# Expert layer of an attention and mixture-of-experts network on 16-bit high and low parts, first product with its weights stationary

## What is computed

```python
def _L0_ffn_ref(x, wg1, bg1, wg2, w_in, w_out):
    E, H, K, G = (8, 512, 2, 64)
    xt = x.reshape(-1, d)                     # 2048 rows, d = 256
    g = jax.nn.gelu(xt @ wg1 + bg1, approximate=False)
    logits = g @ wg2
    probs = jax.nn.softmax(logits, axis=-1)
    top_vals, top_idx = jax.lax.top_k(probs, K)
    gates = jnp.zeros_like(probs).at[jnp.arange(n)[:, None], top_idx].set(top_vals)
    h = jax.nn.gelu(jnp.einsum('nd,edh->enh', xt, w_in), approximate=False)
    o = jnp.einsum('enh,ehd->end', h, w_out)
    y = jnp.einsum('ne,end->nd', gates, o)
...
    x = x + _L0_xattn_ref(_layernorm(x, axis=-1), ctx_768, ...)
    x = x + _L0_ffn_ref(_layernorm(x, axis=-1), L0_ffn_wg1, L0_ffn_bg1, L0_ffn_wg2, L0_ffn_w_in, L0_ffn_w_out)
    x = x + _L1_xattn_ref(_layernorm(x, axis=-1), ctx_768, ...)
    x = x + _L1_ffn_ref(_layernorm(x, axis=-1), L1_ffn_w_gate, L1_ffn_w_up, L1_ffn_w_down)
```

## Time and profile before

| | us |
|---|---|
| median of 3 runs | 1109.73 |
| lowest and highest | 1107.92, 1112.27 |
| the profiled execution | 1105.96 |
| its span (first to last instruction) | 1104.2 |
| expert layer: first DMA, first matmul of the tile loop, last `copy_y`'s start | 524.27, 584.27, 722.02 |
| PE busy in the span | 914.9 (83%) |
| DVE, ACT, POOL busy | 782.2, 745.7, 623.5 |

### The profile page before, as it was taken

How to read it: one execution, slowest core, us unless ns; L and a number is a source line. 1 busy time by engine, 2 the same in 40 slices (tenths; PEclk the granted TensorE clock), 3 DMA queues, 4 the chain that set the end, 5 groups by cost and what they waited for, 6 DMA issues and landing times. The chain is left out here.

```text
span 1104.2 us, 23943 instructions
## 1 busy us (share of the span) xinstructions
PE 914.9 (83%) x9014; PEld 698.9 (63%) x9014; DVE 782.2 (71%) x1550; ACT 745.7 (68%) x1254; POOL 623.5 (56%) x571
## 2 busy tenths in 40 slices
PE   5887998999999999997518999967888989960686
PEld 4655686767676777675417999955566767760344
DVE  5768778777877786676894444458978786639676
ACT  3387888698878887882533444445797878924686
POOL 2177766776686666772515555333686767813232
PEclk9899999999999999998758999988998999975899
DMA  9479999899989979994912222182899979943011
GB/s 265 164 127 193 160 157 152 153 171 151 163 145 184 158 149 152 149 175 65 321 67 73 77 75 75 58 282 43 173 187 173 168 145 172 173 78 114 6 35 39
DMA packets 433744, 153.57 MB, mean 139 GB/s; under 512 B 406592, under 2 KB 424192, under 8 KB 433600
## 3 DMA queue, kind: packets, MB, share of 16 engines
q1 hardware_dynamic: 429888, 141.82, 66.6%
q0 software_dynamic: 3744, 10.23, 2.9%
HBM read 38.62 MB, written 12.71 MB: 46 GB/s over the span
## 5 line engine op out<-in xcount | busy, mean ns | idle before, releaser
L477 POOL TENSOR_TENSOR A_PHL<-A_pr,A_PHL 128x508 f16<-128x508 f32 x256 | 295.2, 1159 | 134.5 <-ACT A_pr L754 133.6
L753 ACT ACTIVATE A_PHL<-A_ps,A_negmax 128x508 f16<-128x508 f32 x256 | 179.6, 701 | 17.9 <-DVE A_negmax L1003 15.3
L477 POOL TENSOR_TENSOR C_PHL<-C_pr,C_PHL 128x512 f16<-128x512 f32 x128 | 150.5, 1186 | 58.0 <-ACT C_pr L754 57.5
L754 ACT ACTIVATE A_pr<-A_ps,A_negmax 128x508 f32<-128x508 f32 x256 | 181.5, 709 | 0.0
L1003 DVE TENSOR_REDUCE A_negmax<-A_ps 128x2 f32<-128x1016 f32 x128 | 154.3, 1205 | 0.0
L598 PE MATMUL A_ps<-A_K,A_Q 64*128 64x512 f32 x768 | 124.1, 427 | 12.4 <-ACT A_pr L754 9.8
L616 PE MATMUL A_ps<-A_VH,A_PT 128*128 128x65 bf16 (+1 forms) x1024 | 109.5, 197 | 18.9 <-DMA A_PT<-A_PHL 18.6
L616 PEld LDWEIGHTS A_ps<-A_VH,A_PT 128*128 128x128 f16 (+1 forms) x1024 | 93.6, 98 | 47.7 <-DMA A_PT<-A_PHL 29.6
L617 PE MATMUL A_ps<-A_VL,A_PT 128*128 128x64 f16 (+1 forms) x1024 | 108.6, 194 | 0.0
L618 PE MATMUL A_ps<-A_VH,A_PT 128*128 128x65 bf16 (+1 forms) x1024 | 108.3, 195 | 0.0
L753 ACT ACTIVATE C_PHL<-C_ps,C_negmax 128x512 f16<-128x512 f32 x128 | 88.7, 693 | 15.1 <-DVE C_negmax L1003 14.5
(11 more groups left out here) (355 smaller groups left out, 2681.8 us busy)
## 6 DMA issues: line engine op xcount, KB each, us to landing
A_PT<-A_PHL SPq DMA_TRANSPOSE x256, 3.4
M_WINl<-in_L_ffn_w_in SPq DMA_DIRECT2D x4, 1024.0 KB, 11.9
M_WOUTl<-in_L_ffn_w_out SPq DMA_DIRECT2D x4, 1024.0 KB, 12.5
C_yc<-routed_rows SPq DMA_DIRECT2D x8, 512.0 KB, 5.2
ct_split<-A_CT SPq DMA_DIRECT2D x4, 768.0 KB, 4.1
C_CT<-ct_split SPq DMA_DIRECT2D x4, 768.0 KB, 8.0
M_rows<-M_xn SPq DMA_DIRECT2D x4, 512.0 KB, 9.0
out<-X SPq DMA_DIRECT2D x16, 128.0 KB, 1.7
```

The costliest lines, as they stand in the source:

```text
L477: pool.tensor_tensor(PHL[:, e % PRING, 1, 0:KEYS], pr[:, e % RING, 0:KEYS], PHL[:, e % PRING, 0, 0:KEYS], ALU.subtract).then_inc(pl_ready. ...
L753: a.activation(PHL[:, e % PRING, 0, 0:KEYS], o, ACT.Exp, bias=nm[:, n % 4, h:h + 1])
L754: a.activation(pr[:, e % RING, 0:KEYS], o, ACT.Exp, bias=nm[:, n % 4, h:h + 1]).then_inc(p_ready.sem, 1)
```

## The change

The weights' parts become 16-bit (high float16, low bfloat16). They no longer are split in place: the loads go to a ring `raw` of 8 parts (4 loads), and loads 4 to 7 wait until earlier parts are split. The rows are split while they still lie in SBUF (`xhl`, 8 pairs of tiles), and turned by 8 DMA transposes on SP's queue, two after each of the first four loads; the rows in DRAM are high and low side by side, the same bytes as before. POOL makes 7 of the 16 low parts, DVE 9. In the tile loop a gathered tile (128 x 512, 16 bit) is turned by one DMA transpose on SP (39 of them). `expert_in` takes a 128 x 128 block of `WIN` as the stationary operand, at a register address, and moves the 128 turned rows: 24 matmuls of 128 columns in place of 6 of 512. Its output has the hidden numbers on the partitions, so that `turn_h` goes; ACT and DVE split it from SBUF. `expert_out` keeps its 12 matmuls of 256 columns, now 16-bit. PE does expert_in(s), expert_out(s-2).

```diff
-    RING, AHEAD = 3, 4
+    RING, AHEAD, XRING, HRING, IN_BANKS = 4, 4, 4, 3, 3
+    OUT_LAG, BACK_LAG = 2, 3
+    RAWS, PAIRS, SETS = 8, TILES // 2, 4
...
-        rows = nc.dram_tensor(f"{tag}_rows", [TILES * P, D], F32).ap()
+        rows = nc.dram_tensor(f"{tag}_rows", [TILES * P, 2 * D], F16).ap()
...
-        WIN = [sb(f"WIN{s}", [P, E, KC, H], FR) for s in "hl"]
-        WOUT = [sb(f"WOUT{s}", [P, E, HC, D], FR) for s in "hl"]
+        WIN = [sb(f"WIN{s}", [P, E, KC, H], dt) for s, dt in (("h", F16), ("l", BF16))]
+        WOUT = [sb(f"WOUT{s}", [P, E, HC, D], dt) for s, dt in (("h", F16), ("l", BF16))]
+        raw = sb("raw", [P, RAWS, KC * H], F32)
...
-        BY_POOL = 6
+        BY_POOL = (0, 1, 2, 4, 6, 8, 10)
...
+            def load_w(k):
+                (W, name), e = LOADS[k]
+                if k >= RAWS // PAIR:
+                    n = PAIR * (k - RAWS // PAIR + 1)
+                    sp.wait_ge(w_split, lows(n, True))
+                    if lows(n, False):
+                        sp.wait_ge(w_split_v, lows(n, False))
+                j = PAIR * k % RAWS
+                sp.dma_start(raw[:, j:j + PAIR, :].rearrange("p e (c n) -> p e c n", n=w[name].shape[3]),
+                             w[name][e:e + PAIR].rearrange("e p c n -> p e c n")).then_inc(w_loaded[k % SETS], 16)
+
+            def turn_rows(p):
+                sp.wait_ge(rows_split, p + 1)
...
+                sp.dma_start_transpose(out=XT[:, b % 2, t:t + 2, :, :].rearrange("p t k n -> p (t k) n"),
+                                       in_=xhl[:, 2 * p:2 * p + 2, :, :].rearrange("p t s d -> p (t s d)")).then_inc(xt_loaded[p % SETS], 16)
...
+            def turn_x(i):
+                sp.wait_ge(xg_loaded[i % AHEAD], 16 * (i // AHEAD + 1))
+                if i >= XRING:
+                    sp.wait_ge(in_filled, i - XRING + 1)
+                sp.dma_start_transpose(out=xgT[:, i % XRING, :, :], in_=xg[:, i % AHEAD, :]).then_inc(gt_loaded[i % XRING], 16)
+
+            for i in range(NT):
+                turn_x(i)
...
+            def expert_in(i):
+                expert[i] = pe.value_load(etab[0:1, i:i + 1], min_val=0, max_val=E - 1)
+                pe.wait_ge(gt_loaded[i % XRING], 16 * (i // XRING + 1))
+                if i >= IN_BANKS:
+                    pe.wait_ge(h_ready, i - IN_BANKS + 1)
+                for c in range(HC):
+                    for kc in range(KC):
+                        last = three(ps[:, IN_BANK + i % IN_BANKS, c * P:(c + 1) * P],
+                                     [a[:, bass.ds(expert[i], 1), kc, c * P:(c + 1) * P].rearrange("p o n -> p (o n)") for a in WIN],
+                                     [xgT[:, i % XRING, s * KC + kc, :] for s in range(2)], kc == 0, kc == KC - 1)
+                last.then_inc(in_filled, 1)
...
-            for s in range(NT + 3):
+            for s in range(NT + OUT_LAG):
                 if s < NT:
-                    turn_in(s)
-                if 1 <= s <= NT:
-                    expert_in(s - 1)
-                if 2 <= s <= NT + 1:
-                    turn_h(s - 2)
-                if s >= 3:
-                    expert_out(s - 3)
+                    expert_in(s)
+                if s >= OUT_LAG:
+                    expert_out(s - OUT_LAG)
...
+            def h_high(i):
+                a.wait_ge(h_ready, i + 1)
...
+                a.activation(hhl[:, i % HRING, 0, :].bitcast(BF16), hf[:, i % HRING, :], ACT.Copy).then_inc(h_hi, 1)
...
             def h_low(i):
-                v.wait_ge(ht_hi, i + 1)
...
+                v.wait_ge(h_hi, i + 1)
+                v.tensor_tensor(hhl[:, i % HRING, 1, :], hf[:, i % HRING, :], hhl[:, i % HRING, 0, :].bitcast(BF16),
+                                ALU.subtract).then_inc(h_split, 1)
```

More of the change, by code:

```diff
@@ L1139, in mixture @@
         xn_ready = sem("xn_ready")
+        rows_hi = sem("rows_hi")
+        rows_split = sem("rows_split")
         rows_stored = sem("rows_stored")
-        xt_filled = sem("xt_filled")
-        xt_hi = sem("xt_hi")
-        xt_split = sem("xt_split")
+        xt_loaded = [sem(f"xt_loaded{k}") for k in range(SETS)]
         z_filled = sem("z_filled")
@@ new lines, in _ @@
+            load_w(0)
+            turn_rows(0)
+            turn_rows(1)
+            load_w(1)
+            turn_rows(2)
+            turn_rows(3)
+            load_w(2)
+            turn_rows(4)
+            turn_rows(5)
+            load_w(3)
+            turn_rows(6)
+            turn_rows(7)
+            for b in range(B):
+                store_rows(b)
+            for k in range(4, len(LOADS)):
+                load_w(k)
+            def turn_x(i):
[3 more added lines that the diff above has]
+                sp.dma_start_transpose(out=xgT[:, i % XRING, :, :], in_=xg[:, i % AHEAD, :]).then_inc(gt_loaded[i % XRING], 16)
@@ L1237, in _ @@
                 gather(i)
-            pool.wait_ge(table_ready, 1)
-            for s in range(NT + 4):
+            pool.wait_ge(table_ready, 3)
+            for s in range(NT + BACK_LAG):
                 if s + AHEAD < NT:
                     gather(s + AHEAD)
-                if s >= 4:
-                    scatter(s - 4)
+                if s >= BACK_LAG:
+                    scatter(s - BACK_LAG)
         @block.tensor
@@ L1329, in expert_in @@
-            def expert_in(i):
-                pe.wait_ge(gt_split, i + 1)
-                if i >= 2:
-                    pe.wait_ge(h_ready, i - 1)
-                for kc in range(KC):
-                    last = three(ps[:, IN_BANK + i % 2, :], [a[:, i % 2, kc, :] for a in xgT],
-                                 [a[:, bass.ds(expert[i], 1), kc, :].rearrange("p o n -> p (o n)") for a in WIN],
-                                 kc == 0, kc == KC - 1)
-                last.then_inc(in_filled, 1)
@@ L1351, in expert_out @@
                 for c in range(HC):
-                    last = three(ps[:, Y_BANK + i % 2, 0:D], [a[:, i % 2, c, :] for a in hT],
+                    last = three(ps[:, Y_BANK + i % 2, 0:D],
+                                 [hhl[:, i % HRING, 0, c * P:(c + 1) * P].bitcast(BF16), hhl[:, i % HRING, 1, c * P:(c + 1) * P]],
                                  [a[:, bass.ds(expert[i], 1), c, :].rearrange("p o n -> p (o n)") for a in WOUT],
@@ L1430, in _ @@
+            for s in range(NT):
+                gelu(s)
+                h_high(s)
             a.wait_ge(l_sub, 1)
@@ L1484, in _ @@
             ch.link(v.tensor_scalar(y.bitcast(I32), two.bitcast(I32), -1.0, float(0x5F3759DF), ALU.mult, ALU.add))
-            for _ in range(3):
+            row_low(1)
+            normalised(2)
+            for k in range(3):
                 ch.link(v.tensor_tensor(two, y, y, ALU.mult))
```

275 lines of the change are left out of this document (115 added, 160 removed).

## The result

| | us |
|---|---|
| before, median (lowest to highest, 4 runs) | 1108.83 (1104.75 to 1112.27) |
| after, median (lowest to highest, 4 runs) | 1138.18 (1135.26 to 1142.24) |
| ratio after to before, 95% interval | 1.0265, 1.0232 to 1.0297 |
| profiled execution of after, its span | 1135.38, 1133.6 |

The change makes the kernel slower by 2.65%, some 29 us. The forecast was 1115, the range 1108 to 1129. The changed kernel was timed in one call only; where a later run is set against its 1138.18, the two come from different calls.

The account below looks back on a forecast made before the run. PE's sequencer, slowed by register addresses, was to bound the tile loop at 3.65 us a tile; loop +6.8, ahead of it -0.4, end -1.5, together +4.9, gave 1115 us, range 1108 to 1129.

Parts of the forecast that it names:

- The array, the sequencer's mechanism: Tile loop: PE's sequencer needs 3.65 us a tile for register instructions, above the array's 2.65; loop +6.8 us.
- The first rival: Tile loop: register steps overlap, the array stays the bound, 2.7 to 3.0 us a tile, whole 1082; chance 0.11.
- the second: `expert_in`: register-addressed stationary loads at 0.11 a pair, 3.95 us a tile, whole 1126; chance 0.17 together with a shallow queue.
- the tail of the earlier trace: Last tile before the change, PE empty: seven register steps 0.80 to 0.86 us apart, taken as 0.115 a step.
- Ahead of the loop: Loads, eight transposes and stores in turn on the DMA queue, then DVE's chain; loop starts at 583.9, -0.4 us.
- The size of a tile: Tile loop: eight groups 1.89, `expert_out` 0.90, expert read 0.75, semaphore 0.11: 3.65 us, ends 3.54 and 3.95.
- The slow rival ahead of the loop: Ahead of the loop: transposes slower than 1.76 us, sharing DMA engines with loads and stores; +5, whole 1120; chance 0.12.
- The end: After the last `expert_in`: three `expert_out` at 1.31 and 1.05 to the copy's end, 4.9 against 6.4 us; -1.5.
- PE's busy share: Sign in the tile loop: falls from 100% to some 75%, with short idle times before each group put down to issue.

Follow-up runs that it names:

- The runs at fixed addresses: Changed kernel always taking expert 0's weights at a fixed address, in the second product (1101.43 us), the first (1093.18) or both (1089.60).
- the run with the low parts dealt out otherwise: Against the kernel with WG split early, weights moving and PE turning the hidden rows: low parts 9 and 11 later on DVE, 12 on POOL; 1103.28 us.
- WG early: Changed kernel with DVE's two instructions splitting the router's weights moved from behind the seventh pair of rows to behind the second; 1126.64 us, ratio 1.0148.
- the run with both products at fixed addresses: Changed kernel with both expert products always taking expert 0's weights at a fixed address, the expert's read kept on PE; 1089.60 us, one run.

## Why the prediction was wrong

In the profile the expert layer grew by 23.3 us, where +4.9 was forecast. Of the 18.4 us between, 10.3 lie ahead of the loop and 8.1 in it.

**The array, the sequencer's mechanism: right.** The forecast's theory was that the array gets its work too late because of the register instructions, with the array's own price at 2.65 us. The runs at fixed addresses show both: 2.65 with the first product's register work gone, 3.01 with two thirds of all register instructions left, 3.84 with all. The first rival (the array bounds) and the second (dear register-addressed loads) fell. The view was the tail of the earlier trace rows: seven steps with an empty PE.

**Ahead of the loop: the step that failed.** The sum had loads and transposes one behind the other as if the queue always had something to issue, and said of load 4 "it lands at 556.2 to 560.8", that is 31.9 to 36.5 us after the layer's first DMA. It landed after 42.5. The sum left out a wait that the code shows: the transpose of rows 4 needs `z_filled`, the gate's first product, and with it WG's split, which the change put behind nearly all of DVE's row work; and SP has loads 3 to 7 queued behind that wait. Moving two small DVE instructions brought load 4 to 36.5 and gave back 6.2 us of the start. A changed order on one engine has to be read on the engine that waits for it: the price of those two instructions was 0.5 us on DVE and 6 at the loop's start.

The sum has a slip besides: its start of the loop, 580.6 to 585.2, has its middle at 582.9 and not at 583.9, so by its own terms the start was 58.6 after the first DMA. Measured are 69.9, 11.3 more. Load 4 is 8.3 of them (42.5 against the middle of 34.2): 6.0 for the wait, and 2.3 that stay when it is gone, at the late end of the sum's bracket. The other 3.0 are on DVE and were in no term: the low part ahead of `cnt` took 2.30 in place of some 1.2, and one small instruction behind it 2.19 in place of 0.23, both beside a low part on POOL. Of the nine profiles of changed kernels eight have one small DVE instruction between `cnt` and `src_u` at 1.71 to 2.19 us like this, and the run with the low parts dealt out otherwise has three; the two of the kernel before have none there. From `src_u` (593.04) to the first matmul (599.79) it was 6.75 us, forecast 6.7.

**The size of a tile: too small.** 3.65 was forecast, 3.84 measured, inside the stated 3.54 to 3.95; over 38 tiles that is 7 of the 8.1 us by which the loop passed the forecast. Each term of the sum holds to 0.01 us. What the sum lacks are single steps that take longer now and then: in the timeline above, the third matmul stands 0.14 behind the second at 641.40 in place of 0.06. The tail had a little of it in view: its seven steps span 0.83 us, 0.119 each, with one of 0.144 among them, and at 0.119 the sum comes to 3.7; it took the undisturbed steps. A tile that is bound by the sequencer has no slack to take them up. Their cause is open; no run here was made for it.

**The slow rival ahead of the loop** (+5 from slower transposes, at 2.2 us each) had the right place and sign and the wrong mechanism for most of it. The eight transposes took SP 1.24 to 3.21 us each, 15.0 in all, against 9.4 to 14 in the sum and 17.6 in the rival; with WG early, where the wait was gone, they took 14.9. So they were a little slower than the sum had them, which is part of the 2.3 us, and they don't make the 6.0.

**The end: right.** 4.9 us, as forecast.

**PE's busy share: wrong.** It was to fall to some 75%. It fell to 94%, and the starvation shows in the distances of starts only.

**The range** reached to 1129, for dearer loads. It added no case in which two terms were late together, and had +5 as the end of the stretch ahead of the loop. Loop and start together came to +25 in the profile. The layer's excess over the forecast accounts for 1133 of the measured 1138; the rest is of the size by which the first attention scatters.

## What to carry to other kernels

An operand at a new register address cost PE's sequencer 0.11 to 0.12 us here, with 128 columns of stationary operand behind it as with 256 of moving; count these steps beside the columns before a product is cut into smaller matmuls, and take them from a stretch in which PE is empty, since a full PE hides them. Where the operand that changes with the data is used, let each address serve as many columns as it can. And for each wait that a change adds to a queue, list what stands behind it. When work moves between DVE and POOL, look which small DVE instructions of the critical chain then run beside a long one on POOL.

## What the runs showed of the hardware

- A matmul with its load of 128 columns and a register address runs at 0.056 to 0.06 us once the address is there; the step for a new address takes 0.112 to 0.124, with one or with two matmuls in it. In the page "TensorE: Matmul & The Clock Gate", section "Back-to-back issue gap", the Trainium skill gives some 81 ns for each matmul of 128 columns in a stream of loads and matmuls; the run with both products at fixed addresses had 24 of them in 1.34 us, 0.056 each, in tile after tile, so the trace doesn't agree with it, and the measured figure decides.
- A busy share of PE of 94% can stand over a loop in which the array would need 2.65 of 3.84 us.
- Some small DVE instructions end only as a POOL subtraction beside them ends: 1.5 to 2.6 us where the same instructions take 0.2 to 0.8 in other profiles.
- With transposes among the loads the DMA engines were full at 250 to 307 GB/s, with loads and stores alone, in the kernel before, at 364 to 376.
- Single steps of PE's sequencer take longer than their 0.112 to 0.124 us, in the tile above 0.133, 0.170 and 0.215.
- With a second DMA transpose of 128 x 1024 in each tile the DMA share went from 0.41 to 1.09 and the tiles became uneven, 2.60 to 5.90 us.
